# Two attention stages in one program, with the other batch's output and gated stages set between their steps

## The chip, the core and the metric

The kernel runs on one core of a Trainium2 chip. Its time is the device time of one execution in microseconds. The engines are TensorE (PE in the rows, its weight loads PEld), VectorE (DVE), ScalarE (ACT), GpSimd (POOL) and SyncE (SP, which issues most DMAs). They run side by side, each in its own order, and wait for each other by semaphores.

## What is computed

A tensor x of 2 batches x 1024 tokens x 512 features goes through four blocks, each `x = x + layernorm(block(layernorm(x)))`, with float32 in and out:

1. attention of 32 heads of 16, no mask: `softmax(q k^T / 4) v`, then `@ w_o`;
2. a gated feed-forward of width 1376 with integer weights and float scales: `(silu(x @ gate) * (x @ up)) @ down`;
3. attention of 32 query heads on one shared key and value head, with a causal mask and a slope per head, then `@ Wo`;
4. `z = x @ W + b` plus a low-rank product m, clipped by the ratio of their norms.

Attention and feed-forward of the first two blocks need nothing of the other batch. The projection of block 3 needs block 2 of its own batch alone.

## The kernel before

The program is a row of stages with a barrier after each: A (normalise, project q, k, v of block 1), B (attention 1), C (its output product, `output`), D (`gated_ffn`), F (projection for block 3), G (attention 2), H (its output product), I (`adapter_ffn`). Between stages the activations go through DRAM. Every product of float32 operands is three products of rounded parts (high x high, high x low, low x high, `split_product`, lines 73 to 75): a chain of 4 chunks x 3 is 12 matmuls of 128x128 weights by 512 columns into one PSUM bank. ScalarE makes the high parts, VectorE the low ones.

`attention` works on four heads of one batch at a time (16 such groups, `ITS`), in two halves of 512 queries ("turns", 32 in all) and, in a turn, in steps of 128 keys: 8 steps per turn in B (256 steps in all), 4 and 8 in causal G (192 steps). A step does this:

- `key_scores` (L793): the scores of 128 keys by 512 queries for 4 heads, one matmul each, into one of three banks `st_ps`. It uses only half of PE's rows: heads 0 and 1 lie in rows 0 to 63, heads 2 and 3 in rows 64 to 127, so two matmuls of different halves can run together. In G's diagonal steps two mask matmuls follow each (L804).
- `exps` (L720): ScalarE takes the exponential of each bank into `probs`.
- `values` (L826): the probabilities of the step before, times values with a column of ones, for 4 heads side by side in 32 columns each, summed in `o_ps`.
- `row_scores` (L782): the same scores with queries as rows, for a coming turn, into four banks `s_ps`, two per head and 128 queries; VectorE takes the maximum of each pair of banks in one scan (L755 in B, L752 with the mask in G). When a turn's maxima are there, PE turns them (L814), ScalarE and GpSimd split them in two parts and SP copies them as rows into `q_stack`.

The order within a step is planned in Python: `plan_units` spreads the scans over the steps in proportion to the work with a lead (`LEAD`), `step_order` alternates the two halves of PE's rows. On PE a step is: scores in that order, then the values of the step before.

C turns the outputs on PE (L894), scales by the sums, turns back (L902), splits, multiplies by w_o and normalises; D keeps all its split weights in SBUF and takes them once; F projects.

## Time and profile before

| | us |
|---|---|
| median of 3 runs (lowest, highest) | 2242.59 (2234.47, 2245.1) |
| the profiled execution | 2230.07 |
| its span, first to last instruction | 2228.3 |
| mean granted PE clock | 0.936 of full |
| PE, DVE, ACT, POOL busy | 1996.4, 1454.2, 1151.9, 134.4 |

The span falls into 0 to 221 us (A and the start of B up to its first step), 221 to 906 (B's steps), 906 to 1532 (C, D, F and the start of G), 1532 to 2016 (G's steps), 2016 to 2105 (H) and the rest (start and body of I). PE's busy time counts a matmul from issue to a modelled end, so neighbours overlap in it, and 99% busy is not the same as streaming all the time: the distance between starts says more.

### The profile page before, as it was taken

What the parts mean: (1) busy time and instruction counts of PE and PEld (TensorE: products, weight loads), DVE (VectorE), ACT (ScalarE), POOL (GpSimd) and SP (SyncE); (2) the same over time, 40 slices, a digit from 0 to 9 for tenths busy, and PEclk for the clock granted to TensorE, in tenths of its full rate; (3) what the DMA queues carried; (4) which work ended last, traced back from release to release, by engine and by line L of the source; (5) the groups of instructions that cost most, each with busy time, mean ns of one, the idle gap of its engine ahead of it and who ended that gap; (6) DMA issues with size and microseconds to landing.
All of it is one profiled execution on the core that took longest, in us unless ns stands there. A gap on an engine that the chain in (4) does not pass through costs nothing. (4 is left out here: it accounts for less than half of the span.)

```text
span 2228.3 us, 31983 instructions
## 1 busy us (share of the span) xinstructions
PE 1996.4 (90%) x12048; PEld 1151.6 (52%) x12048; DVE 1454.2 (65%) x2484; ACT 1151.9 (52%) x2431; POOL 134.4 (6%) x171
## 2 busy tenths in 40 slices
PE   7995999999999999869999998668999999998685
PEld 5772333333333333557888886454444444446564
DVE  5315899999999995464434233537777777835677
ACT  3220788888888887213322221223777777762153
POOL 0000000000000000120010010000000000001213
PEclk9995999999999999888999999786999999987898
DMA  6445233233233220244010100442332222202411
GB/s 220 161 147 73 35 53 45 39 50 48 39 49 49 39 35 2 76 146 127 17 38 1 39 19 5 169 125 49 50 49 46 42 42 46 50 2 95 147 45 69
DMA packets 97705, 143.57 MB, mean 64 GB/s; under 512 B 28900, under 2 KB 40036, under 8 KB 97408
## 3 DMA queue, kind: packets, MB, share of 16 engines
q1 hardware_dynamic: 96440, 139.35, 26.6%
q10 hardware_dynamic: 728, 1.41, 0.4%
q8 instruction: 95, 1.56, 0.3%
q0 software_dynamic: 384, 0.77, 0.2%
q14 instruction: 58, 0.48, 0.1%
HBM read 93.91 MB, written 47.05 MB: 63 GB/s over the span
## 5 line engine op out<-in xcount | busy, mean ns | idle before, releaser
L755 DVE TENSOR_REDUCE maxesB<-s_psB 128x1 f32<-128x1024 f32 x512 | 602.4, 1218 | 91.7 <-PE s_psB L782 91.6
L720 ACT ACTIVATE probsB<-st_psB 128x512 f32<-128x512 f32 x1024 | 529.0, 602 | 132.7 <-PE st_psB L793 132.6
L752 DVE CUSTOM_DVE_ANT_0 junkG<-s_psG,ramp 128x896 bf16<-128x896 f32 (+7 forms) x512 | 367.7, 755 | 120.2 <-PE s_psG L782 108.5
L793 PE MATMUL st_psB<-q_stackB,k_stackB 50*128 50x512 f32 x1024 | 410.5, 478 | 8.3 <-DMA q_stackB<-mpartsB 4.4
L720 ACT ACTIVATE probsG<-st_psG 128x512 f32<-128x512 f32 (+3 forms) x768 | 325.6, 492 | 115.8 <-PE st_psG L804 62.7
L782 PE MATMUL s_psB<-k_stackB,q_stackB 48*128 48x512 f32 x1024 | 354.8, 455 | 27.5 <-DMA k_stackB<-k_parts 20.5
L793 PEld LDWEIGHTS st_psB<-q_stackB,k_stackB 50*128 50x128 f32 x1024 | 169.8, 187 | 277.7 <-ACT probsB L720 235.4
L793 PE MATMUL st_psG<-q_stackG,k_stackG 54*128 54x512 f32 (+3 forms) x768 | 264.0, 419 | 22.2 <-ACT probsG L720 16.2
L782 PE MATMUL s_psG<-k_stackG,q_stackG 52*128 52x512 f32 (+3 forms) x768 | 255.8, 422 | 29.7 <-DMA q_stackG<-bias_copy 17.2
L826 PE MATMUL o_psB<-probsB,v_onesB 128*32 128x512 f32 x2048 | 279.3, 618 | 0.0
L782 PEld LDWEIGHTS s_psB<-k_stackB,q_stackB 48*128 48x128 f32 x1024 | 158.5, 191 | 116.9 <-DVE maxesB L755 86.7
L782 PEld LDWEIGHTS s_psG<-k_stackG,q_stackG 52*128 52x128 f32 x768 | 131.0, 193 | 117.0 <-DVE maxesG L752 69.7
L793 PEld LDWEIGHTS st_psG<-q_stackG,k_stackG 54*128 54x128 f32 x768 | 128.6, 189 | 110.9 <-ACT probsG L720 79.5
L826 PE MATMUL o_psG<-probsG,v_onesG 128*32 128x512 f32 (+3 forms) x1536 | 169.9, 516 | 0.0
L1128 DVE SCALAR_TENSOR_TENSOR hD<-u_psD,suD,siluD 128x512 f32<-128x512 f32 (+1 forms) x44 | 33.0, 750 | 203.0 <-PE u_psD L75 200.7
L804 PE MATMUL st_psG<-masks,halves 64*128 64x64 bf16 (+1 forms) x1024 | 120.6, 212 | 0.0
L1088 ACT ACTIVATE siluD<-g_psD,sgD 128x512 f32<-128x512 f32 (+1 forms) x44 | 30.3, 688 | 132.2 <-PE g_psD L75 132.1
L1096 ACT ACTIVATE hhD<-hD 128x512 fp32r<-128x512 f32 (+1 forms) x44 | 27.8, 632 | 118.4 <-DVE hD L1128 118.4
L826 PEld LDWEIGHTS o_psB<-probsB,v_onesB 128*32 128x32 f32 x2048 | 40.8, 109 | 64.7 <-ACT probsB L720 34.2
L73 PE MATMUL g_psD<-xhTD,wg_highD 128*128 128x512 f32 (+1 forms) x176 | 70.5, 400 | 1.4 <-DVE xlTD L170 1.4
L75 PE MATMUL g_psD<-xhTD,wg_lowD 128*128 128x512 f32 (+1 forms) x176 | 70.6, 401 | 0.0
L73 PE MATMUL y_psD<-wd_highD,hhD 128*128 128x512 f32 (+1 forms) x176 | 70.1, 398 | 0.0
(240 smaller groups left out, 2818.1 us busy)
## 6 DMA issues: line engine op xcount, KB each, us to landing
q_stackB<-q_parts SPq DMA_DIRECT2D x93, 128.0 KB
k_stackB<-k_parts SPq DMA_DIRECT2D x93, 128.0 KB
q_stackG<-q_parts SPq DMA_DIRECT2D x93, 128.0 KB
q_parts<-partsA SPq DMA_DIRECT2D x16, 512.0 KB, 2.8
k_parts<-partsA SPq DMA_DIRECT2D x16, 512.0 KB, 2.8
q_parts<-partsF SPq DMA_DIRECT2D x16, 512.0 KB, 2.8
k_stackG<-k_parts SPq DMA_DIRECT2D x93, 64.0 KB
xA<-in_x SPq DMA_DIRECT2D x4, 1024.0 KB
```

The source lines that it names most:

```text
L73: pe.matmul(out, left[0], right[0], start=start, stop=False)
L75: return pe.matmul(out, left[1], right[0], start=False, stop=stop)
L720: act.activation(probs[:, (i % ring) * GH + h, first:HALF], st_ps[:, n % n_st, first:HALF], ACT.Exp).then_inc(st_used, 1)
L752: dve.tensor_tensor_reduce(junk[:, n % JUNK, 0:width], scores, ramp[:, SEQ - width:SEQ], 1.0, LOWEST, ALU.add, ALU.max, out).then_inc(maxe ...
L755: dve.reduce_max(out, scores, AX.X).then_inc(maxed, 1)
L782: ins = pe.matmul(s_ps[:, slot_of[n] + part, 0:b - a], qst[at, it % 3, half, h % GS, qt * P:(qt + 1) * P], kst[at, it % 3, h % kh, a:b], s ...
L793: ins = pe.matmul(st_ps[:, n % n_st, first:HALF], kst[at, it % 3, h % kh, kt * P:(kt + 1) * P], qst[at, it % 3, half, h % GS, first:HALF], ...
L804: ins = pe.matmul(st_ps[:, n % n_st, first:first + wide], halves[at, a, :], masks[at, a, 0:wide], start=False, stop=a == 1)
L826: ins = pe.matmul(o_ps[32 * h:32 * h + 32, first:HALF], vone[:, it % 2, kt, h % vh, :], probs[:, (i % ring) * GH + h, first:HALF], start=k ...
L1088: act.activation(silu[0:k, :], g_ps[0:k, :], ACT.Silu, scale=sg[0:k, j:j + 1]).then_inc(silu_out, 1)
L1096: act.activation(hh[0:k, c % 2, :], h[0:k, :], ACT.Copy).then_inc(hh_out, 1)
L1128: dve.scalar_tensor_tensor(out=h[0:k, :], in0=u_ps[0:k, :], scalar=su[0:k, j:j + 1], in1=silu[0:k, :], op0=ALU.mult, op1=ALU.mult).then_in ...
```

## The change

Attention 1 and attention 2 become one list of 448 steps in one stage (`class Attention`): batch 0 and then batch 1 of block 1 (steps 0 to 127, 128 to 255), then batch 0 and batch 1 of block 3 (256 to 351, 352 to 447). Stages C (without its scaling), D and F are cut into units (`class Middle`): "o" one output tile, "t" turning a normalised tile, "g" and "u" a gate and an up product, "d" a group of up to four down products per 128 output columns, "b" turning the result back, "s" and "v" the second projection. A full unit is 12 matmuls. Per batch there are 8 o, 16 t, 22 g, 22 u, 24 d, 8 b, 10 s and 2 v. Batch 0's units stand in steps 140 to 230, batch 1's in steps 268 to 334, one or two per step in the first and one to three in the second.

In such a "filled" step PE does half of the scores, half of the unit products, the rest of the scores, the rest of the products, then the values. Eight PSUM banks are shared: in filled steps the row scores have two banks instead of four, the key scores two instead of three, the units three; each row scan is then two scans of 512 columns with a maximum to join them. `probs` holds two steps instead of four.

Further edits: the attention's outputs go to DRAM and come back packed, with reciprocals of the sums by two more DMA hops and a GpSimd product (`divide`), so nothing is turned on PE for it; silu is made from tanh in three operations; 1/sqrt is a power on GpSimd; gate, up, down and projection weights are fetched per use (82 pieces of 128 x 512 per batch, four landing places), converted to float and reduced to the low part on GpSimd and to the high part on ScalarE. H (`class Output`) is in the same program without a barrier before it, without the turning. A and I are as they were.

```diff
+FILLS = ((140, 231), (268, 318))
-JUNK = 8
+JUNK = 2
...
+        def give(key, ring, wide, release):
+            allowed = {"row": ([0, 1], [0, 1, 2, 3]), "take": ([4, 5], [4, 5, 6]), "fill": ([2, 3, 6],) * 2}[key[0]][not ring]
...
+            cuts = [(0, min(HALF, width)), (HALF, width)] if halved[t] else [(0, width)]
...
+class Middle:
+    def schedule(self, b, first, last):
+        order = [("o", b, t) for t in range(KT)] + [("t", b, 0, 0, i) for i in range(TB)]
...
+        for n, unit in enumerate(order):
+            early = after(unit)
+            if n >= 3:
+                old = mine[n - 3]
+                early = max(early, at[old] + (2 if old[0] in "ob" else 1))
...
+        elif kind in "gu":
+            ins = split_product(pe, bank[0:k_, :], self.parts(p, every, slice(k_ * g, k_ * (g + 1))),
+                                (self.xT[:, 0, g, :], self.xT[:, 1, g, :]), g == 0, g == n_groups - 1)
...
+        @block.vector
+            for i in range(steps):
+                early = att.scans_before_cut(i)
+                for n in early:
+                    att.maximum(dve, n)
+                mid.vector_middle(dve, i)
+                for n in att.scans_at[i][len(early):]:
+                    att.maximum(dve, n)
+                att.vector_step(dve, i)
+                mid.vector_last(dve, i)
...
+        @block.scalar
+            for i in range(steps):
+                mid.scalar_first(act, i)
+                att.exps(act, i, slice(0, GH // 2))
+                mid.scalar_middle(act, i)
+                att.exps(act, i, slice(GH // 2, GH))
+                att.scalar_step(act, i)
+                mid.scalar_last(act, i)
...
+        @block.tensor
+            for i in range(steps):
+                cut = att.cut_of(i)
+                att.scores(pe, i, slice(0, cut))
+                mid.front_products(pe, i)
+                att.scores(pe, i, slice(cut, None))
+                mid.back_products(pe, i)
+                if i:
+                    att.values(pe, i - 1)
+                for t in att.turn_after.get(i, ()):
+                    att.turn_max(pe, t)
```

PE in the middle of attention 1 before: `st_psB` are key scores, `s_psB` row scores, `o_psB` the values; one step from one L826 to the next.

```order
L826 MATMUL o_psB<-probsB,v_onesB 32x512 x4
L793 MATMUL st_psB<-q_stackB,k_stackB 128x512
L782 MATMUL s_psB<-k_stackB,q_stackB 128x512
L793 MATMUL st_psB<-q_stackB,k_stackB 128x512
L782 MATMUL s_psB<-k_stackB,q_stackB 128x512 x2
L793 MATMUL st_psB<-q_stackB,k_stackB 128x512
L782 MATMUL s_psB<-k_stackB,q_stackB 128x512
L793 MATMUL st_psB<-q_stackB,k_stackB 128x512
L826 MATMUL o_psB<-probsB,v_onesB 32x512 x4
```

The second half of a filled step of attention 1 now (its first half is a key score, a row score, a key score and six products like these); L971 are key scores, L959 row scores, L78 to L80 the products of one unit, L1007 the values.

```order
L80 MATMUL banks<-xT_mid,w_mid 128x512
L959 MATMUL banks<-k_stack,q_stack 128x512 x2
L971 MATMUL banks<-q_stack,k_stack 128x512
L959 MATMUL banks<-k_stack,q_stack 128x512
L971 MATMUL banks<-q_stack,k_stack 128x512
L78 MATMUL banks<-xT_mid,w_mid 128x512
L79 MATMUL banks<-xT_mid,w_mid 128x512
L80 MATMUL banks<-xT_mid,w_mid 128x512
L78 MATMUL banks<-xT_mid,w_mid 128x512
L79 MATMUL banks<-xT_mid,w_mid 128x512
L80 MATMUL banks<-xT_mid,w_mid 128x512
L1007 MATMUL banks<-probs,v_ones 32x512 x4
```

The four pairs of a step are cut into three and five matmuls with products between, and the three row scores of the second half stand close together, on two banks.

VectorE in attention 1 before (scans L755, the copy of a finished turn L759), and in filled steps now (scans L919; L1569 and L1595 the gate's and the up product's part of the activation, L1628 its low part).

```order
L755 TENSOR_REDUCE maxesB<-s_psB 128x1 x16
L759 COPY oTB<-o_psB 128x512
L755 TENSOR_REDUCE maxesB<-s_psB 128x1 x16
L759 COPY oTB<-o_psB 128x512
L755 TENSOR_REDUCE maxesB<-s_psB 128x1 x16
```

```order
L1569 SCALAR_TENSOR_TENSOR th_mid<-th_mid,banks 128x512
L919 TENSOR_REDUCE maxes<-banks 128x1 x3
L936 RECIPROCAL o_recip<-o_sums 128x16
L919 TENSOR_REDUCE maxes<-banks 128x1
L1595 SCALAR_TENSOR_TENSOR th_mid<-banks,sc_mid,th_mid 128x512
L919 TENSOR_REDUCE maxes<-banks 128x1 x3
L1628 TENSOR_TENSOR hx_1367<-th_mid,hx_1367 128x512
L919 TENSOR_REDUCE maxes<-banks 128x1
```

The unit's operation stands after the first of four half scans; its low part stands last in the step and waits for ScalarE.

At the end of attention 1 before, the steps have key scores alone, and stage C begins behind the barrier:

```order
L793 MATMUL st_psB<-q_stackB,k_stackB 128x512 x4
L826 MATMUL o_psB<-probsB,v_onesB 32x512 x4
L793 MATMUL st_psB<-q_stackB,k_stackB 128x512 x4
L826 MATMUL o_psB<-probsB,v_onesB 32x512 x8
L627 UNCONDITIONAL_BRANCH
L888 UNCONDITIONAL_BRANCH
L894 MATMUL a_psC<-ident,oTB 128x128 x16
```

The same place now carries the row scores of the first causal turn (narrow ones of 128 and 256 columns):

```order
L1007 MATMUL banks<-probs,v_ones 32x512 x4
L959 MATMUL banks<-k_stack,q_stack 128x512 x2
L959 MATMUL banks<-k_stack,q_stack 128x128
L971 MATMUL banks<-q_stack,k_stack 128x512
L959 MATMUL banks<-k_stack,q_stack 128x128 x2
L971 MATMUL banks<-q_stack,k_stack 128x512
L959 MATMUL banks<-k_stack,q_stack 128x128
L959 MATMUL banks<-k_stack,q_stack 128x256
L971 MATMUL banks<-q_stack,k_stack 128x512 x2
```

Attention 2 no longer starts from nothing.

## Rows read from the trace of the kernel before

**Rows 1.** The page: busy time and share of the span by engine.
```profile
PE 1996.4 (90%) x12048; PEld 1151.6 (52%) x12048; DVE 1454.2 (65%) x2484; ACT 1151.9 (52%) x2431; POOL 134.4 (6%) x171
```

**Rows 2.** Stretches by stage: length, then busy time (count) by engine, granted clock, DMA.
```profile
221.00:906.00 685.00, 676.52 (x4112) 247.14 (x4112) 591.95 (x521) 542.17 (x1086) 23.21 (x46) 0.98 0.28 40
906.00:990.00 84.00, 68.97 (x384) 58.04 (x384) 59.81 (x133) 16.20 (x37) 20.64 (x16) 0.94 0.31 109
...
1008.00:1392.00 384.00, 375.84 (x1632) 302.04 (x1632) 141.43 (x232) 98.17 (x138) 19.33 (x14) 0.98 0.10 30
...
1532.00:2016.00 484.00, 453.81 (x4108) 222.01 (x4108) 346.75 (x960) 351.56 (x862) 17.36 (x46) 0.97 0.24 41
2016.00:2105.00 89.00, 69.63 (x384) 59.23 (x384) 59.60 (x132) 16.80 (x38) 20.63 (x16) 0.88 0.31 109
```

**Rows 3.** Stretches inside the two attentions: steady part and tail of each.
```profile
400.00:500.00 100.00, 99.49 (x620) 36.79 (x619) 91.77 (x82) 80.69 (x163) 3.49 (x7) 1.00 0.30 45
...
866.00:904.00 38.00, 34.25 (x146) 9.44 (x142) 0.72 (x2) 23.80 (x48) 0.45 (x1) 0.70 0.00 1
...
1600.00:1700.00 100.00, 94.04 (x892) 47.57 (x891) 78.28 (x217) 74.59 (x187) 3.83 (x10) 1.00 0.35 54
...
1980.00:2015.00 35.00, 31.96 (x197) 11.76 (x196) 0.00 (x0) 19.48 (x48) 0.45 (x1) 0.65 0.00 1
```

**Rows 4.** Timeline of PE, one step of attention B (start, length, instruction).
```profile
601.23 0.49 PE L793 MATMUL st_psB<-q_stackB,k_stackB 50*128 50x512 f32 x1
601.23 0.49 PE L782 MATMUL s_psB<-k_stackB,q_stackB 48*128 48x512 f32 x1
601.56 0.39 PE L793 MATMUL st_psB<-q_stackB,k_stackB 50*128 50x512 f32 x1
...
602.41 0.49 PE L793 MATMUL st_psB<-q_stackB,k_stackB 50*128 50x512 f32 x1
602.83 0.64 PE L826 MATMUL o_psB<-probsB,v_onesB 128*32 128x512 f32 x4
603.28 0.61 PE L826 MATMUL o_psB<-probsB,v_onesB 128*32 128x512 f32 x4
603.82 0.50 PE L793 MATMUL st_psB<-q_stackB,k_stackB 50*128 50x512 f32 x1
```

**Rows 5.** Timeline of DVE, ACT and PE's loads in the same step.
```profile
601.76 2.07 ACT L720 ACTIVATE probsB<-st_psB 128x512 f32<-128x512 f32 x4 [0.53 <-PE st_psB L793]
...
601.84 0.18 PEld L782 LDWEIGHTS s_psB<-k_stackB,q_stackB 48*128 48x128 f32 x1 [0.31 <-DVE maxesB L755]
...
602.03 2.36 DVE L755 TENSOR_REDUCE maxesB<-s_psB 128x1 f32<-128x1024 f32 x2 [0.24 <-PE s_psB L782]
```

**Rows 6.** Groups by line and form: count, busy us, mean ns of one, idle before.
```profile
L755 DVE TENSOR_REDUCE maxesB<-s_psB 128x1 f32<-128x1024 f32 x512 | 602.4, 1218 | 91.7 <-PE s_psB L782 91.6
L1128 DVE SCALAR_TENSOR_TENSOR hD<-u_psD,suD,siluD 128x512 f32<-128x512 f32 (+1 forms) x44 | 33.0, 750 | 203.0 <-PE u_psD L75 200.7 <-ACT siluD L1088 2.3
L319 POOL TENSOR_TENSOR xD<-xD,yD 128x512 f32<-128x512 f32 x16 | 22.4, 1430 | 385.4 <-DVE yD L311 385.4
L752 DVE CUSTOM_DVE_ANT_0 junkG<-s_psG,ramp 128x512 bf16<-128x512 f32 x64 | 41.6, 689 | 13.6 <-PE s_psG L782 13.6
L678 POOL COPY v_onesB<-v_loadB 128x512 f32<-128x512 f32 x16 | 9.8, 616 | 115.0 <-PE o_psB L826 96.9 <-DMA v_loadB<-v_rows 18.2
L131 DVE TENSOR_SCALAR xnD<-xD,mvD,rstdD 128x512 f32<-128x512 f32 x16 | 7.7, 542 | 0.1
L311 DVE TENSOR_SCALAR yD<-yD,ymvD,yrstdD 128x512 f32<-128x512 f32 x16 | 15.4, 1024 | 0.1
```

**Rows 7.** Timeline of PE: 24 products apart, and 16 transposes at stage C's start.
```profile
154.89 0.39 PE L73 MATMUL acc_psA<-v_highA,xhTA 128*128 128x512 f32 x1
...
160.50 0.39 PE L73 MATMUL acc_psA<-v_highA,xhTA 128*128 128x512 f32 x1
...
906.97 1.94 PE L894 MATMUL a_psC<-ident,oTB 128*128 128x128 f32 x16 [1.60 <-PEq L1430]
```

More of the change, by code:

```diff
@@ new lines, in vector_step, with row_scores @@
+    def vector_step(self, dve, i):
+        t = self.ended(i, 1)
+        if t is not None and t < 2 * ITS:
+            self.vector_copy_o(dve, t)
+        t = self.ended(i, INVERT)
+        if t is not None:
+            self.invert(dve, t)
+    def row_scores(self, pe, n, part):
+        t, qt, h, *_ = self.scans[n]
+        it, half = divmod(t, 2)
+        a, b = self.scan_parts(n)[part]
+        if part == 0:
+            if t % 2 == 0 and (n == 0 or self.scans[n - 1][0] != t):
+                pe.wait_ge(self.stacks, self.stacks_by[it])
+            for free in self.frees["row", n]:
+                pe.wait_ge(*free)
+        at = slice(self.side(h), self.side(h) + MAIN + ALIBI)
+        ins = pe.matmul(self.banks[:, self.bank_of["row", n] + part, 0:b - a],
+                        self.qst[at, it % 3, half, h % GS, qt * P:(qt + 1) * P],
+                        self.kst[at, it % 3, h % GS if it < ITS else 0, a:b], start=True, stop=True)
+        if part == len(self.scan_parts(n)) - 1:
+            ins.then_inc(self.scored, 1)
@@ new lines, in key_scores @@
+    def key_scores(self, pe, i, h):
+        it, half, kt, first, diagonal = self.steps[i]
+        n = self.where["exp", i, h]
+        for free in self.frees["take", n]:
+            pe.wait_ge(*free)
+        at = slice(self.side(h), self.side(h) + MAIN + ALIBI + SHIFT)
+        ins = pe.matmul(self.banks[:, self.bank_of["take", n], first:HALF],
+                        self.kst[at, it % 3, h % GS if it < ITS else 0, kt * P:(kt + 1) * P],
+                        self.qst[at, it % 3, half, h % GS, first:HALF], start=True, stop=not diagonal)
+        if not diagonal:
+            ins.then_inc(self.st_made, 1)
@@ new lines, in values @@
+    def values(self, pe, i):
+        it, half, kt, first, _ = self.steps[i]
+        t = 2 * it + half
+        if i == self.first_of[t] and half == 0:
+            pe.wait_ge(self.v_set, it + 2)
+        if kt == 0 and t:
+            pe.wait_ge(self.o_out, t)
+        pe.wait_ge(self.st_used, max(self.exps_of[i]) + 1)
+        for h in range(GH):
+            ins = pe.matmul(self.banks[32 * h:32 * h + 32, 7, first:HALF], self.vone[:, it % 2, kt, h if it < ITS else 0, :],
+                            self.probs[:, i % 2 * GH + h, first:HALF], start=kt == 0, stop=i + 1 == self.first_of[t + 1])
+        ins.then_inc(self.pv_done, 1)
@@ new lines, in tensor_ahead, with scores @@
+    def tensor_ahead(self, pe):
+        pe.wait_ge(self.fixed, 16 * 2 * SIDES)
+        for n in self.before:
+            for part in range(len(self.scan_parts(n))):
+                self.row_scores(pe, n, part)
+        for t in self.early_turns:
+            self.turn_max(pe, t)
+    def scores(self, pe, i, items):
+        if items.start in (None, 0) and i == self.first_of[2 * self.steps[i][0] + self.steps[i][1]]:
+            pe.wait_ge(self.m_rows, self.N_ROWS * (2 * self.steps[i][0] + self.steps[i][1] + 1))
+        for kind, *which in self.orders[i][items]:
+            if kind == "row":
+                self.row_scores(pe, *which)
+            elif kind == "key":
+                self.key_scores(pe, i, *which)
+            else:
+                self.mask_keys(pe, i, *which)
@@ L1387, in one @@
         def one(i):
[L1388 removed]
+            return slice(i, i + 1)
         def store_parts(scratch, j):
```

1732 lines of the change are left out of this document (1062 added, 670 removed).

## The prediction

> **What bounds the kernel now.** I read the page first. PE is busy 90% of the span, DVE 65%, ACT 52%, POOL 6% [rows 1], so the time is PE's or that of whoever holds PE up. The stretches by stage come next [rows 2]: in attention B PE is busy 677 of 685 us, in D 376 of 384, in G 454 of 484, in H 70 of 89. Between C, D, F and G the barriers leave PE with little. Then the steady part of each attention [rows 3]. A step of B has 16.25 PE records (4 key scores, 4 row scores, 8 for the values, 2 per 8 steps for the turned maxima), so 620 in 100 us are 38.2 steps: 2.62 us per step. G has 260 records per 12 steps: 892 in 100 us are 41.2 steps: 2.43 us per step.
>
> The timeline of one step says how much of the 2.62 us PE needs [rows 4]. Two pairs of scores start 0.33 us apart, the last key score to the values takes 0.42, the two rounds of values 0.45 and 0.54: (603.82 - 602.83) = 0.99 us. Four pairs at 0.33, plus about 0.2 ahead of the values, plus 0.99 is 2.5 us. DVE has two scans in 2.36 us and ACT four exponentials in 2.07 [rows 5]. So there is 0.1 us of slack per step for foreign products, and 12 products between steps will lengthen them by nearly their whole length. The change can gain only what stands outside the steps, and it pays for cutting steps in two.
>
> **The cost of the units.** Products start 0.234 us apart at full clock: 24 in 160.50 - 154.89 = 5.61 us [rows 7]. A batch has 8 o + 22 g + 22 u + 16 full d + 10 s = 78 units of 12 and 8 of 9 products: 1008 products, 236 us. Its turning (t, b, v) is 104 small transposes at 1.94 / 16 = 0.12 us [rows 7]: 12.5 us. Together 248.5 us per batch, 497 for both.
>
> **The cost of a filled step of attention 1.** From the order on PE: first half, a pair (0.33), a key score alone (0.21) and a switch to the full array; six products; second half, two row scores (a pair), a key score, the third row score, the last key score; products; values 0.99. Two costs are new.
>
> First the third row score of the second half. It reuses the bank of the first one, whose scan must be over. From the issue of a row score to its scan: 602.03 - 601.56 = 0.47 us, the pair at 601.56 being the second of its head [rows 4, 5]. A scan of 512 columns was not run in B; the same width in G took 0.689 [rows 6], half of B's 1.218 would be 0.61; I take 0.69. From the end of a scan to the next load I take 0.04. So 1.20 us from the first row score to the third, and PE has two matmuls between them, 0.56 us: a stall of 0.64 us. Before, with four banks, the same wait was 0.31 us of a load whose neighbour went on [rows 5].
>
> Second the switches. The values use all rows in 32 columns, scores half the rows in 128 columns, products the whole array. The second round of values to the next score took 0.54 against 0.45 between the rounds: 0.09 us more; score to values took 0.42 against the 0.21 of its columns: 0.2 more [rows 4]. Before there are two such changes per step, now five. I take 0.1 for each added one, 0.3 per step; the ends are 0 and 0.6. The Trainium skill, TensorEngine Tiling (Array Packing), Key Properties, says that changing the tiling mode drains TensorE; by this rule the added changes cost something each, and the 0.09 and 0.2 agree.
>
> A filled step without its products is then 0.54 + 0.56 + 0.64 + 0.33 + 0.99 + 0.3 and the last key score's 0.1 of exposed load = 3.46 us, against 2.62. 91 steps: 315 us, plus 248.5 of units = 563; two more steps keep the narrow bank rings at about 3.2 us each: 6. 163 steps stay at 2.62: 427.
>
> **A filled step of attention 2.** Its scores are cut four and four with the pairs kept, its scans are short (128 to 512 columns), two row scores stand in each half and the first half's scans are over when six or more products have passed. I add 0.3 for switches and 0.07 for the rest: 2.8 us. 69 steps: 193 us, plus 248.5. Here a unit's bank is the one freed by the unit three before, and in 17 places that one stood in the step just before and is freed by an operation that DVE does only after this step's first scans: about 0.47 + 1.1 + 0.75 (the operation, 750 ns in D [rows 6]) against 1.0 of scores: 1.3 us each, 22; with smaller ones in the second halves 27. Sum 469. The other 123 steps at 2.43: 299.
>
> **What goes.** 906 to 1532 us (626 us: C, D, F, three starts behind barriers and G's start) go as a whole; their products are counted above. B's last 38 us hold 146 records, 12.2 steps of 12, worth 32 us; PE's granted clock was 0.70 there after it had less to do [rows 3]. These steps now carry the next layer's row scores at the full clock. Of the 14 us by which B's 685 exceed 256 steps at 2.62, I let 8 stand (the start). G's 484 exceed 192 steps at 2.43 by 17; its tail (35 us for 11.4 steps, clock 0.65 [rows 3]) stays, the start goes: 12 stand. H loses its turning and scaling and its start: 16 tiles of 12 products at 0.234 are 45 us, DVE needs about 2.7 per tile beside that, 8 us until the last turn's sums are back by DMA (DVE stands in line for them), 12 us from the last product to I's first work as now: 65 instead of 89. I's 123 us and A's 221 stay, with 5 more at the start, since SP alone issues all stacks and GpSimd more constant rows.
>
> **Cover.** Costs that I put at nothing, since PE has 6.2 us in a filled step of attention 1: DVE has four half scans (2.76) and on average 1.5 for units, ACT 2.07 and 1.1 for units and weights, POOL 0.9 pieces of a copy and a subtraction (616 ns for a copy, 1430 for a two-input operation [rows 6]): 1.8 and little else. Where POOL runs late, PE's wait for low weights is behind it, and everything in PE's order behind that. DMA brings 82 pieces of 0.26 MB in 569 us, 38 GB/s beside the 40 of attention B [rows 2]; stage C alone moved 109.
>
> **Sum.** 226 + 427 + 8 + 569 + 299 + 12 + 469 + 65 + 123 = 2198 us against 2228.3: 30 less, 1.3%. The profiled execution took 2230.07, 12.5 below the median of 2242.59; on the median's scale the forecast is 2212 us.
>
> **Rivals.** (a) PE hides its own waits. If the third row score's scan is earlier than I think (0.61 us scans, or a gap filled by reordered loads), switches cost nothing and bank waits vanish, then 58 + 47 + 27 = 132 us come off: 2080. For it: PE's loads are pulled ahead of waiting matmuls in rows 4 and 5. Against it: 0.20 before the values is in every step. Half of it gives 2146.
>
> (b) Slower: the hand-over of a filled step becomes a loop through three engines. h is made by DVE, its high part by ACT behind four exponentials, its low part by DVE as the last work of the step; the next step's first scan is behind that on DVE, and its end frees the bank that PE's second-half row score wants. By the durations above the low part ends 0.5 us before PE's next step, and another 1.0 us of lateness is absorbed until the second half. If DVE comes later than that, PE waits with it. An operation of POOL beside DVE's two-input one can do this: a `TENSOR_SCALAR` of 128x512 took 542 ns where GpSimd idles (L131) and 1024 where it adds rows at the same time (L311), though L311 also writes in place [rows 6]. One POOL operation of 1.43 us in the way of each step, 0.6 of it covered, is 0.8 x 158 = 126 us more: 2338. It decides from 0.19 us per filled step, where my 30 us are gone. The Trainium skill, SBUF — State Buffer, Who interferes with whom, says that a VectorE operation with two SBUF inputs and a GpSimd one that reads SBUF exclude each other for a whole instruction. By it L1628 would wait behind POOL's weight work; no run here shows this pair.
>
> (c) Weights come late. SP stands in one line for maxima, stacks, turns and 164 pieces, each piece needing the low part of the fourth before it. If each costs PE 0.5 us: 82 us more, 2294. For it: SP issues take 0.4 to 0.5 us and block on semaphores. Against it: pieces are asked for five steps ahead, some 30 us.
>
> That units aren't where they should be is excluded by the order.
>
> **Chances.** Forecast (2170 to 2250) 0.37; (a) 0.28; (b) 0.22; (c) 0.08; something else on the slow side 0.05. The range of 8 in 10 is 2100 to 2320. Within 0.5% (2231 to 2254), which a measurement of this kernel can't tell from no change, 0.15; faster 0.60 (all of (a), most of the forecast's width), slower 0.25.
>
> **What would show it.** In the changed profile: unfilled steps of 2.62 and 2.43 us; filled steps of attention 1 at 3.46 us plus 2.81 per unit; PE's waits for the scan before the third row score of 0.6 us about 90 times, some 58 us; no stretch of PE below full clock between the first step and attention 2's tail; H at about 65. Wrong: PE waiting for low weights (c), or DVE busy or waiting for ACT and POOL in filled steps with PE waiting for DVE over 1 us each (b), or filled steps near 2.9 us plus units (a).

## The result, and the profile after

The changed kernel took 2610.87 us (median of 4 runs, 2597.68 to 2615.69) against 2239.35 us for the kernel before (2234.47 to 2245.1): a ratio of 1.167, 95% interval 1.162 to 1.171. The forecast was 2212 us, the range 2100 to 2320, and slower had a chance of 0.25. It is 399 us off and outside the range. Now and then an execution takes clearly longer than the others of the same kernel; medians and ratios here leave such ones out.

The page of the changed kernel answers [rows 1]. The second row is the granted clock in 40 slices of the span:
```profile
PE 2205.2 (84%) x11728; PEld 1178.9 (45%) x11728; DVE 1488.7 (57%) x2924; ACT 1215.5 (47%) x2536; POOL 516.3 (20%) x624
PEclk9986999998699889987689889889978678785888
```
PE has fewer matmuls than before (11728 against 12048) and is busy 209 us longer. No other engine is near its limit. What differs is PE's clock: the mean granted clock is 0.866 against 0.936, and 704 us of the span lie at the level 0.5 (1.2 GHz), against 288 us before.

The stretches by stage answer [rows 2, 3]. They are, in this order: unfilled steps of attention 1, its filled steps, unfilled steps around the change to attention 2, filled steps of attention 2, its unfilled ones, H. Columns as in rows 2:
```profile
235.66:609.53 373.87, 361.02 (x2244) 133.28 (x2242) 336.64 (x326) 295.04 (x590) 23.59 (x35) 1.00 0.41 74
609.53:1326.77 717.24, 619.63 (x2625) 310.24 (x2624) 382.52 (x651) 304.90 (x574) 196.23 (x239) 0.86 0.27 61
1326.77:1433.21 106.44, 93.25 (x644) 39.98 (x642) 78.77 (x179) 72.82 (x156) 5.51 (x10) 0.91 0.41 87
1433.21:2005.68 572.47, 491.76 (x2608) 306.83 (x2606) 273.16 (x809) 222.84 (x489) 196.29 (x238) 0.88 0.29 70
2005.68:2417.34 411.66, 330.29 (x2360) 157.41 (x2362) 195.91 (x552) 208.05 (x498) 28.78 (x42) 0.73 0.29 59
2417.34:2490.00 72.66, 51.06 (x204) 36.46 (x196) 42.10 (x81) 11.65 (x18) 36.39 (x33) 0.85 0.27 95
```
Set beside the forecast's pieces, with the third stretch split at 1397.14 us, where attention 1's last values start. The same cuts, made at the first value product of a step, were made in the traces of the experiments below (one step later around the filled steps of e7, e10 and e12, whose units start later; the numbers hold to some 2 us). All in us of the profiled run; "at 0.5" is the time of the whole span at that granted clock:

| | forecast | after | e1 | e5 | e7 | e10 | e12 |
|---|---|---|---|---|---|---|---|
| start | 226 | 236 | 237 | 236 | 237 | 241 | 241 |
| attention 1, unfilled | 435 | 444 | 452 | 455 | 484 | 439 | 438 |
| attention 1, filled | 569 | 717 | 718 | 571 | 562 | 560 | 564 |
| attention 2, unfilled | 311 | 448 | 373 | 421 | 371 | 377 | 374 |
| attention 2, filled | 469 | 572 | 574 | 567 | 562 | 566 | 548 |
| H and I | 188 | 196 | 195 | 197 | 198 | 198 | 198 |
| sum | 2198 | 2614 | 2549 | 2446 | 2413 | 2381 | 2363 |
| at 0.5 | | 704 | 614 | 506 | 479 | 455 | 418 |

The surplus of 416 us has three main parts: 148 in the filled steps of attention 1, 137 in the unfilled ones of attention 2, 103 in its filled ones. They hold 200, 233 and 133 us of the time at 0.5.

**What a filled step does.** Four waits, over the whole span (waiting engine and line, what ended the wait, us in total, times, longest):
```profile
PE banks L959 <- DVE maxes L919: 93.0, 137, 4.1
PE banks L959 <- DVE maxes L916: 93.8, 48, 18.7
DVE o_recip L936 <- DMA o_sums<-turns: 139.0, 22, 26.6
PE banks L78 <- POOL w_mid L1452: 6.5, 2, 3.5
```
L959 is a row score, L919 and L916 are the scans of attention 1 and 2, L936 is `invert`, L1452 makes the low part of the weights. Of the first row 82.0 us lie in the filled steps of attention 1; of the third 94.6 us lie in attention 2's last unfilled steps. Step 174 of attention 1 shows the first row. PE's row scores, and DVE from the step's first scan to the last ones, from the timeline:
```profile
889.99 0.49 PE L959 MATMUL banks<-k_stack,q_stack 52*128 52x512 f32 x1
890.32 0.68 DVE L919 TENSOR_REDUCE maxes<-banks 128x1 f32<-128x512 f32 x1
890.92 0.67 DVE L1569 SCALAR_TENSOR_TENSOR th_mid<-th_mid,banks 96x512 f32<-96x512 f32 x1
891.06 0.50 PE L959 MATMUL banks<-k_stack,q_stack 52*128 52x512 f32 x1 [0.58 <-DVE maxes L919]
...
891.70 0.75 DVE L1595 SCALAR_TENSOR_TENSOR th_mid<-banks,sc_mid,th_mid 96x512 f32<-96x512 f32 x1
892.37 0.53 DVE L1611 TENSOR_SCALAR xn_mid<-x_mid,xmv_mid,xrstd_mid 128x512 f32<-128x512 f32 x1
892.82 1.96 DVE L919 TENSOR_REDUCE maxes<-banks 128x1 f32<-128x512 f32 x3
893.55 0.50 PE L959 MATMUL banks<-k_stack,q_stack 52*128 52x512 f32 x1 [2.00 <-DVE maxes L919]
...
895.32 0.79 PE L959 MATMUL banks<-k_stack,q_stack 52*128 52x512 f32 x1
```
The step's first scan stands ahead of DVE's work for the units, the other three behind it. The row score at 893.55 wants the bank of a row score whose scan is the first behind 1.9 us of unit work, and PE waits 2.00 us for it. The next row scores take 0.79 us instead of 0.50: the granted clock went to 0.5 at 894.6 and came back at 911.6. So a wait of 2 us was followed by 17 us at half the clock. That this wait alone lowered it isn't shown: the step holds only four transposes for its unit, and PE had been busy 7.34 of the 10 us before 894.
```profile
884.00:894.00 10.00, 7.34 (x39) 3.58 (x37) 5.61 (x10) 3.67 (x8) 1.50 (x3) 1.00 0.10 23
895.00:907.00 12.00, 10.35 (x36) 4.21 (x32) 7.45 (x12) 5.68 (x12) 1.72 (x4) 0.50 0.16 48
```

**What an unfilled step of attention 2 does.** Step 359, all of SP's turn work and what waits long (SPq rows are DMA issues):
```profile
2101.26 0.57 SPq L764 DMA_DIRECT2D o_packed<-turns  x1
2101.87 0.56 SPq L767 DMA_DIRECT2D o_sums<-turns  x1
...
2108.83 0.25 DVE L936 RECIPROCAL o_recip<-o_sums 128x16 f32<-128x16 f32 x1 [8.55 <-DMA o_sums<-turns]
...
2110.06 0.76 PE L959 MATMUL banks<-k_stack,q_stack 52*128 52x512 f32 x1 [7.78 <-DVE maxes L916]
```
DVE has come to the reciprocal at 2100.3, before the sums' fetch is issued, and goes on 7 us after the issue. The scans stand behind it in DVE's order, so PE waits 7.78 us. The two stretches around it, before and behind 2106 us:
```profile
2086.00:2106.00 20.00, 15.92 (x134) 8.17 (x129) 8.69 (x24) 10.95 (x30) 6.07 (x8) 0.83 0.32 68
2106.00:2140.00 34.00, 29.33 (x165) 14.14 (x166) 17.29 (x51) 14.43 (x32) 3.57 (x4) 0.55 0.16 34
```
34 us at 0.55 follow. The row of attention 2 in [rows 3] had 1.00.

### The profile page after: what moved, and what is told of

Its sections match the earlier page's. It is cut to its first block and busy times, and to the rows that moved or that the text cites. A ratio compares the mean times of both kernels' runs of the same rounds, so it can differ in the third digit from the quotient of the medians.

```text
span 2613.7 us, 34456 instructions
## 1 busy us (share of the span) xinstructions
PE 2205.2 (84%) x11728; PEld 1178.9 (45%) x11728; DVE 1488.7 (57%) x2924; ACT 1215.5 (47%) x2536; POOL 516.3 (20%) x624
## 5 line engine op out<-in xcount | busy, mean ns | idle before, releaser
L885 ACT ACTIVATE probs<-banks 128x512 f32<-128x512 f32 (+3 forms) x1792 | 887.5, 553 | 938.8 <-PE banks L971 616.4
L959 PE MATMUL banks<-k_stack,q_stack 52*128 52x512 f32 (+3 forms) x1792 | 686.0, 479 | 225.6 <-DVE maxes L916 93.8
L919 DVE TENSOR_REDUCE maxes<-banks 128x1 f32<-128x512 f32 (+1 forms) x720 | 630.8, 911 | 351.4 <-PE banks L959 350.4
L971 PE MATMUL banks<-q_stack,k_stack 54*128 54x512 f32 (+3 forms) x1792 | 751.4, 482 | 30.7 <-ACT probs L885 16.8
L916 DVE CUSTOM_DVE_ANT_0 junk<-banks,ramp 128x512 bf16<-128x512 f32 (+7 forms) x608 | 380.9, 660 | 374.8 <-PE banks L959 361.3
L959 PEld LDWEIGHTS banks<-k_stack,q_stack 52*128 52x128 f32 x1792 | 309.9, 206 | 489.7 <-DVE maxes L919 203.5
L971 PEld LDWEIGHTS banks<-q_stack,k_stack 54*128 54x128 f32 x1792 | 333.0, 208 | 382.4 <-ACT probs L885 213.7
L1007 PE MATMUL banks<-probs,v_ones 128*32 128x512 f32 (+3 forms) x3584 | 500.5, 635 | 0.0
L1452 POOL TENSOR_TENSOR w_mid<-land_mid,w_mid 128x512 fp32r<-128x512 f32 (+3 forms) x180 | 206.9, 1165 | 474.3 <-ACT w_mid L1531 474.0
L78 PE MATMUL banks<-xT_mid,w_mid 128*128 128x512 f32 (+1 forms) x432 | 196.8, 456 | 30.1 <-DVE th_mid L1595 13.9
L79 PE MATMUL banks<-xT_mid,w_mid 128*128 128x512 f32 (+1 forms) x432 | 180.4, 418 | 0.0
L80 PE MATMUL banks<-xT_mid,w_mid 128*128 128x512 f32 (+1 forms) x432 | 180.1, 417 | 0.0
L1007 PEld LDWEIGHTS banks<-probs,v_ones 128*32 128x32 f32 x3584 | 74.1, 113 | 120.2 <-issue 77.1
L78 PEld LDWEIGHTS banks<-xT_mid,w_mid 128*128 128x128 f32 (+1 forms) x432 | 86.1, 199 | 83.9 <-issue 32.1
L80 PEld LDWEIGHTS banks<-xT_mid,w_mid 128*128 128x128 f32 (+1 forms) x432 | 87.0, 201 | 21.7
L936 DVE RECIPROCAL o_recip<-o_sums 128x16 f32<-128x16 f32 x64 | 15.9, 248 | 139.0 <-DMA o_sums<-turns 139.0
L79 PEld LDWEIGHTS banks<-xT_mid,w_mid 128*128 128x128 f32 (+1 forms) x432 | 87.2, 202 | 14.2
L78 PE MATMUL banks<-hx,w_mid 128*128 128x512 f32 (+1 forms) x176 | 83.1, 472 | 12.0 <-DVE xT_mid L1582 4.9
```

Source lines behind the costliest of these rows:

```text
L78: pe.matmul(out, left[0], right[0], start=start, stop=False)
L79: pe.matmul(out, left[0], right[1], start=False, stop=False)
L80: return pe.matmul(out, left[1], right[0], start=False, stop=stop)
L885: act.activation(self.probs[:, i % 2 * GH + h, first:HALF], self.banks[:, self.bank_of["take", n], first:HALF], ACT.Exp).then_inc(self.st_ ...
L916: dve.tensor_tensor_reduce(self.junk[:, n % JUNK, 0:b - a], scores, self.ramp[:, SEQ - width + a:SEQ - width + b], 1.0, LOWEST, ALU.add, A ...
L919: dve.reduce_max(out, scores, AX.X).then_inc(self.maxed, 1)
```

## The experiments

Times are medians, ratios are to the kernel before on the same chip. The kernel before took 2231 to 2236 us in them.

**e1: the sums are not waited for.** One operand and one wait of `invert`; the products are then divided by wrong sums.
```diff
-        dve.wait_ge(self.s_moved, 16 * (t + 1))
+        dve.wait_ge(self.v_set, 1)
...
-        dve.reciprocal(self.fewer[:, t % 2, :], self.few[:, t % 2, :])
+        dve.reciprocal(self.fewer[:, t % 2, :], self.fixed_sums[:, :])
```


> The changed kernel with one data dependence left out: DVE's reciprocal reads a constant tile of ones and no longer the sums that come back by DMA, so its outputs lack the division by the right sums. Every store, fetch, reciprocal and copy of the round trip is still issued. Theory 1 (DVE stands in order for the sums' DMA, 139 us in 22 waits; PE then waits for scans; after each stall PE runs for 10 to 17 us at the granted clock 0.5): the waits and most of the 231 us at low clock in the unfilled steps of attention 2 go; these 123 steps fall from 449 to 300-330 us, the whole to 2330-2420. Theory 2 (filled steps and sparse units lower the clock by themselves, the waits for the sums only stand where PE was late anyway): filled attention 1 stays at 700 or more, the whole stays above 2480. Theory 3 (SP is late with stacks, maxima and weights): little changes, 2550 or more.

Measured: 2550.93 us, ratio 1.143 (1.136 to 1.151). My first theory explains 60 us of the 370, against the 190 to 280 that it expected. It is right about its place: attention 2's unfilled steps fell from 448 to 373 us, and their low clock with them:
```profile
616.76:1334.90 718.14, 621.04 (x2625) 310.79 (x2625) 382.39 (x651) 304.79 (x574) 195.49 (x238) 0.86 0.27 60
2017.11:2353.67 336.56, 296.46 (x2360) 146.77 (x2362) 197.07 (x553) 204.70 (x498) 28.83 (x42) 0.84 0.35 72
```
The first row, the filled steps of attention 1, is what it was (717.24 and clock 0.86): the larger surplus is there, and it is not the sums.

**e2: the reciprocal later.** Whole computation.
```diff
-STORE_TURN, FETCH_TURN, INVERT, STORE_INVERSE, SPREAD_INVERSE, DIVIDE = 2, 4, 6, 7, 9, 11
-FILLS = ((140, 231), (268, 318))
+STORE_TURN, FETCH_TURN, INVERT, STORE_INVERSE, SPREAD_INVERSE, DIVIDE = 2, 4, 9, 10, 11, 13
+FILLS = ((142, 231), (270, 315))
```


> The whole computation. The reciprocal stands 9 steps behind the end of a turn instead of 6 (store of it 10, spread 11, division 13; the units of each batch start 2 steps later). Theory 1: the fetch is issued early enough in SP's order for most turns, so the waits for the sums fall from 139 to under 40 us and the time to 2350-2450. Theory 2: above 2500. Theory 3 (SP itself is behind by more than three steps): the waits move with it, above 2550.

Measured: 2563.7 us, ratio 1.146 (1.139 to 1.153), within its noise of e1. The two are made up differently: in e2 some 55 us of waits for the sums are left (28 of them in the last one), attention 2's unfilled steps fell as in e1 (374 us), attention 1's filled ones came to 697, and its unfilled ones rose from 444 to 489. The value I gave theory 1 was wrong in both.

**e3: the sums in the products' layout.** The stores and spreads of the inverses are gone, DVE inverts 128x512 elements once per two turns.
```diff
-        sp.dma_start(self.few[:, t % 2, :], ...)
+        sp.dma_start(self.inverse[at, slot, :], self.turns[t].rearrange("h s c q -> s h c q")[1])
...
-        dve.reciprocal(self.fewer[:, t % 2, :], self.few[:, t % 2, :])
+        dve.reciprocal(self.inverse[:, slot, :], self.inverse[:, slot, :])
```


> The whole computation with a shorter round trip: the sums, which stand 16 times in the turn anyway, are fetched in the layout of the products, DVE inverts them there 9 steps behind the turn (32 times 128x512, some 0.6-3 us each, instead of 64 times 128x16), and the stores and spreads of the inverses are gone (128 DMAs fewer for SP). Theory 1: waits for the sums under 20 us, 2330-2430. Theory 3 (SP's line): a gain as well, but without one in e1 and e2. Theory 2: above 2500. If the reciprocal of 128x512 takes 3 us, 32 times 2.5 us more of DVE show as stalls and give back up to 80 us.

Measured: 2645.27 us, ratio 1.186 (1.177 to 1.195), slower than the changed kernel. The new operation costs 3.35 us, where 16 columns took 0.25:
```profile
L926 DVE RECIPROCAL o_inverse<-o_inverse 128x512 f32<-128x512 f32 x32 | 107.1, 3346 | 54.6 <-DMA o_inverse<-turns 54.6
```
Its 107 us stand for the 16 us of the 64 small ones, 91 more; against e1 it lost 94. It can't say what the shorter trip is worth.

**e4: a pause in the kernel before.** Attention 2 of the kernel before, 15 times.
```diff
+                if causal and n and n % (2 * UNITS) == 0:
+                    for j in range(7):
+                        dve.reduce_max(spare[:, at + j:at + j + 1], ramp[:, :], AX.X)
                 dve.wait_ge(scored, n + 1)
```


> The kernel before, whole computation, with a pause of DVE of seven 1024-wide maxima of a constant tile (about 8.4 us by the 1.218 us of such a scan in attention 1) at the first scan of every tile pair of attention 2: 15 pauses, once per 12 steps, as often as the changed kernel stalls there. Its own price, less some slack: 7 us each, 105 in all, so 2345 if a stall costs only its length. Theory 1 (the granted clock falls to 0.5 after a stall and stays there 10 to 17 us): 4 to 7 us more behind each, 2400-2450, with stretches at 0.5 behind each pause. Theory 2 (the clock is lowered by what the changed kernel's steps are like): no fall of the clock here.

Measured: 2408.53 us, ratio 1.078 (1.073 to 1.084): 177 us, 11.8 per pause. One pause, and the stretch of attention 2 that holds nearly all of them:
```profile
1660.82 7.97 DVE L750 TENSOR_REDUCE spareG<-ramp 128x1 f32<-128x1024 f32 x7
...
1669.05 0.58 PE L787 MATMUL s_psG<-k_stackG,q_stackG 52*128 52x256 f32 x1 [7.57 <-DVE maxesG L757]
```
```profile
1555.00:2130.00 575.00, 453.11 (x3551) 226.43 (x3548) 428.53 (x964) 310.23 (x739) 15.20 (x40) 0.77 0.19 32
```
The same attention in the kernel before:
```profile
1555.00:1990.00 435.00, 407.91 (x3813) 202.71 (x3812) 331.47 (x912) 323.24 (x796) 16.23 (x43) 1.00 0.25 42
```
PE's wait is 7.6 us, the price 11.8. Over the whole span PE's waits for these scans rose from 9.1 to 116.5 us, 107 of the 177; the other 70 go with the time at 0.5, which rose from 27 to 279 us in attention 2. So a wait costs its length and then the low clock behind it, in a kernel that has nothing of the change, though 70 us for 252 more us at the low level is less than the half that a clock at half speed could cost.

**e8: a short pause.** As e4 with three maxima, 3.6 us.

> The kernel before, whole computation, with three instead of seven maxima in each of the 15 pauses of DVE (3.4 us each by their own rows in e4; e4's of 8.0 us cost 11.8 us each). Attention 2 has some 0.4 to 1 us of slack per pause. If a stall of PE of 2.5 to 3 us also lowers the clock for some microseconds, the cost is 4 to 7 us each, 60 to 105 us, so 2290-2335; if only long stalls do it, 2.5 us each: 2265-2275.

Measured: ratio 1.054 (1.047 to 1.061), some 120 us or 8 per pause of 3.6; its four runs lay between 2342 and 2424 us, wide apart, so only the rough size (7 us per pause even by the shortest) is to be taken from it. It is over both expectations: the price of a pause is about double its length. Short waits are not cheap ones.

**e5: two row scores on each side of the units.** The cut of a filled step moves one item on, behind the second row score; DVE's unit work then stands behind two scans. Whole computation.
```diff
-        return [n for n, item in enumerate(order) if item[:1] + item[2:] == last][GH // 2 - 1] + 1
+        cut = [n for n, item in enumerate(order) if item[:1] + item[2:] == last][GH // 2 - 1] + 1
+        rows = [n for n, item in enumerate(order) if item[0] == "row"]
+        if len(rows) == 4 and sum(n < cut for n in rows) == 1 and rows[1] == cut:
+            cut += 1
+        return cut
```


> The changed kernel, whole computation; in a filled step of four half scans the cut moves behind the second row score (two row scores and their scans stand ahead of the units, two behind, instead of one and three), so that no row score waits for a scan that stands behind DVE's unit work. Theory 4 (short waits of 0.6 to 2 us of PE for the scans inside filled steps, each followed by 3 to 10 us of granted clock 0.5): PE's waits for the scans of attention 1's filled steps fall from about 79 us to under 25, low clock there from 200 us to about 100, the whole by 90 to 130 us: 2480-2525. Theory 5 (PE's clock falls in steps that hold only transposes or nothing, whatever the waits): the waits go but the low clock stays, 2550-2590. The sums' round trip (theory 1, worth 58 us by e1) is left as it is.

Measured: 2449.88 us, ratio 1.097 (1.094 to 1.100): 161 us off, over theory 4's own expectation. PE's waits for the scans in the filled steps of attention 1, in the changed kernel and in e5 (L919 has become L923), and e5's stretch of these steps:
```profile
PE banks L959 <- DVE maxes L919: 82.0, 101, 4.1
```
```profile
PE banks L963 <- DVE maxes L923: 9.8, 15, 2.9
```
```profile
615.14:1185.71 570.57, 537.33 (x2625) 280.16 (x2624) 372.25 (x651) 295.65 (x574) 195.44 (x238) 0.95 0.34 76
```
The same 2625 matmuls in 571 instead of 717 us, the clock at 0.95 instead of 0.86. The waits are 72 us shorter. The time at 0.5 fell from 200 to 58 us, which at half speed is worth up to 71: together 143 of the 147. Theory 5 expected the low clock to stay. It went, though the steps that hold only transposes are still there, so these steps don't lower the clock by themselves; e6 shows that they have a part in it.

**e6: more work for PE.** 20 constant bf16 products ahead of the transposes of each of the 48 turning units.
```diff
+            self.extra(pe, bank)
             for c in range(DC):
                 ins = pe.transpose(bank[:, P * c:P * (c + 1)], self.xn[:, n % 2, P * c:P * (c + 1)], self.ident[:, :])
```


> The changed kernel, whole computation, with work added: 20 products of a constant bf16 tile (128x128 by 128x256, an estimate from the mask products' rows is 0.11 us each at full clock) ahead of the transposes of each of the 48 units that only turn a tile, some 2.2 us each, 105 us of PE work in all, where PE's steps are sparse. Theory 5: the clock stays up there, steps of 7.8 us at half clock become 6.2, and the whole comes out at or under 2614 in spite of the added work (2570-2620). Theory 4: the waits for scans are partly filled by the products (they let DVE catch up), so the added work costs 20 to 60: 2630-2670. If clock and waits are untouched: 2700 or more.

Measured: 2613.26 us, ratio 1.170 (1.165 to 1.176): 960 more matmuls, and no difference from the changed kernel. That is theory 5's expectation (2570 to 2620), and under theory 4's. Five steps with a transposed tile or nothing (146 to 150), of the changed kernel and then of e6:
```profile
672.03:710.00 37.97, 28.07 (x103) 10.19 (x106) 23.54 (x46) 14.58 (x29) 10.88 (x14) 0.55 0.30 43
```
```profile
674.80:708.50 33.70, 27.27 (x179) 14.62 (x178) 22.86 (x45) 13.96 (x27) 10.87 (x14) 0.95 0.31 41
```
With 76 more matmuls recorded they take some 4 us less, at 0.95 instead of 0.55. DVE's work is the same. All filled steps of attention 1, and PE's waits for the scans in them:
```profile
610.89:1319.77 708.88, 619.45 (x3105) 337.36 (x3104) 382.13 (x651) 304.11 (x574) 195.69 (x238) 0.95 0.27 61
```
```profile
PE banks L959 <- DVE maxes L919: 72.7, 99, 2.4
```
The waits are nearly all there (72.7 us of 82.0), and the clock stands at 0.95, as in e5. So the waits for the scans alone don't lower the clock either: taking them away (e5) keeps it up, and so does filling the sparse steps around them (e6). And e6 gives the clock's price by itself. Its time at 0.5 in this stretch fell by 136 us, worth up to 68; its 480 added products are some 53 us by the 0.11 expected of each; measured, 8 us less. In attention 2's filled steps the same sum is 31 against 53, and they got 19 us longer.

**e7: e2 and e5 together.** No new edit.

> The whole computation with e2's later reciprocal and e5's cut together. If the two causes stand side by side their gains add: 2610 - 50 - (e5's gain); by theory 4 2430-2475, by theory 5 2500-2540.

Measured: 2419.98 us, ratio 1.086 (1.081 to 1.090). The gains do not quite add: 30 us beyond e5, where e2 alone had given 47. Attention 1's filled steps stand at 562 us, but its unfilled ones rose to 484, since PE now waits for the maxima's rows (`q_stack<-mparts`), 35.1 us in 10 waits against 10.0 in 7 in e5.

**e10: scans further ahead.** e7 with a longer lead of the scans in attention 1.
```diff
-        ... + (rate * LEAD if t else 0)
+        ... + (rate * (5200 if layer == 0 else LEAD) if t else 0)
```


> Whole computation: e7 (2420), and in attention 1 the scans run further ahead of the steps (5200 columns instead of 3400, some two steps more), so that the maxima's rows have 5 us more to travel. e7's trace has the first step of 7 turns at 5.8 to 7.8 us instead of 2.62, PE waiting up to 5 us for the DMA of the maxima's rows, and low clock behind them. If these waits are that trip: 163 unfilled steps of attention 1 fall from 481 to 435-445 us and the whole to 2375-2390. If they follow the reciprocal, not the rows: 2415-2425.

Measured: 2381.54 us, ratio 1.069 (1.064 to 1.074), as expected: 439 us unfilled, and 4.4 us of waits for these rows.

**e9: GpSimd inverts.** e5 with e3's layout, and a power of -1 on GpSimd in the place of DVE's reciprocal.
```diff
+        pool.tensor_tensor(self.inverse[:, slot, :], self.inverse[:, slot, :], self.minus[:, :].broadcast_to([P, HALF]), ALU.pow)
```


> Whole computation, with e5's cut. As in e3 the sums are fetched in the layout of the products and the stores and spreads of the inverses are gone (128 DMAs fewer), but GpSimd takes them to the power -1 ahead of its multiplication; DVE has no part in the division. 32 operations of 128x512 on GpSimd, whose duration no row shows (128x1 took 0.55 us). Against e5 (2450): if the power takes under 5 us, DVE's wait goes and SP is relieved, 2370-2410; if it takes 10 us or more it stands ahead of GpSimd's weight work and maxima, and the time is over 2450.

Measured: 4583.94 us, ratio 2.054 (2.049 to 2.060). One such operation takes 82 us:
```profile
L833 POOL TENSOR_TENSOR o_inverse<-o_inverse,minus 128x512 f32<-128x512 f32 x32 | 2621.5, 81922 | 67.9 <-DMA o_inverse<-turns 67.9
```
It says nothing on SP's relief.

**e11: stacks of the second batch early.** e7, with attention 2 of the second batch reading the first one's parts.
```diff
-            if it >= ITS and it % NG == 0:
+            if it == ITS:
...
-                return k_parts[1][c, one(it // NG % BATCH)].rearrange("b d (j t) -> (b d) j t", j=1)
+                return k_parts[1][c, one(0)].rearrange("b d (j t) -> (b d) j t", j=1)
...
-            late = {ITS + NG * b: mid.ends[b] + 3 for b in range(BATCH)}
+            late = {ITS: mid.ends[0] + 3}
```


> e7 with one dependence left out: attention 2 of the second batch reads the first batch's parts, so its stacks can be loaded early (its output is wrong). e7's trace has two stalls in the unfilled steps, 16.9 us at step 339 and 17.8 at 351, with PE waiting for the DMA of k_stack, and 32 us at low clock around them. If the late projection of the second batch is the cause: both steps fall to 2.5-4 us, 29 us and some clock, 2380-2395 against 2420. If SP's line is: it stays within 10 us of 2420.

Measured: 2414.96 us, ratio 1.084 (1.080 to 1.088), 5 us from e7. The stall of step 339 went (16.9 to 4.0 us), that of step 351 stayed (16.4 us, PE waiting 12.0 for `k_stack`). So the first of the pair hangs on the late projection. The second doesn't; that it hangs on when SP loads the next stack is likely, but no run shows it. Attention 2's unfilled steps got some 15 us shorter, and attention 1's unfilled steps and H 10 us longer; why wasn't followed.

**e12: one unit behind three.** e10, in 15 steps.
```diff
         half = (len(todo) + 1) // 2
+        if len(self.at(i)) == 1 and len(self.at(i - 1)) >= 3:
+            half = 0
```


> Whole computation: e10 (2382), and in the 15 steps of attention 2 that hold one unit behind a step of three, all its 12 products stand in the second half of the step. e10's trace has such a step (288) at 9.35 us against 5.61: PE waits 2.3 us for DVE's third gating operation, which frees the last of the three unit banks, and runs 3.4 us at the granted clock 0.5 behind it. If that hand-over is what makes attention 2's filled steps 97 us longer than forecast: PE's waits before L78 there fall by 20 to 25 us, low clock from 142 to about 100, and the whole to 2335-2350. If the low clock comes from the rest of the steps, the waits go and come back later: 2370-2385.

Measured: 2371.84 us, ratio 1.061 (1.058 to 1.064). That is the second of the two outcomes I had written down: some waits go and others come. The filled steps of attention 2 fell from 566 to 548 us. In e10, step 288 shows the wait that was removed:
```profile
1442.99 0.50 PE L78 MATMUL banks<-xT_mid,w_mid 128*128 128x512 f32 x1 [2.30 <-DVE th_mid L1599]
1443.33 0.40 PE L79 MATMUL banks<-xT_mid,w_mid 128*128 128x512 f32 x1
...
1444.28 0.63 PE L79 MATMUL banks<-xT_mid,w_mid 128*128 128x512 f32 x1
```
PE's waits for `th_mid` in this stretch fell from 17.7 to 4.9 us, but those for the scans and for ACT rose by 11 us together. Some 80 us above the forecast stay there: 66 us of waits, where the forecast had 27, and 113 us at the low clock. The waits are short, up to 2.9 us, and spread over several releasers; no run takes them away.

**e13: e12 and 12 added products per turning unit.**

> Whole computation: e12 with 12 of e6's constant products (about 0.11 us each) ahead of the transposes of each of the 48 turning units, 63 us of added PE work. In e6 such steps stayed at full clock at 5.2 to 6.2 us with 20 products. If PE's idle time there is a fall of the clock waiting to happen: 10 to 30 us less than e12, 2310-2335. If e5's cut has already taken away what lowered the clock there, the added work only costs: 10 to 40 us more than e12.

Measured: 2391.38 us, ratio 1.070 (1.066 to 1.075): about 20 us more than e12 for some 60 us of work. Time at 0.5 fell from 418 to 352 us, the time didn't. Once e5's waits are gone, the clock that useless work holds up pays back two thirds of the work and no more.

No version came under the kernel before. The fastest, e12, does the changed kernel's work in 239 us less.

## Why the prediction was wrong

- **Start and H.** 236 against 226, H and I 196 against 188. Right to 20 us together.
- **Unfilled steps of attention 1.** 444 against 435: right.
- **A filled step of attention 1 as such.** Forecast 3.46 us and 2.81 per unit. Without the 0.64 us for the third row score that is 5.63 us for a step with one unit and 8.44 with two. With that wait taken out, e5 and e7 measured 5.5 and 8.2 us in such steps where the clock was full. So the order, the switches together and the products were priced right; that e7 and e10 came to 562 and 560 us, near the 569, is partly chance, since 58 us of the 569 are a stall that they don't have, and other waits and 48 us at the low clock took its place. The term of 0.64 us was not right: the same steps of the changed kernel took 6.5 and 9.25 us at full clock, 1.0 more. I took the distance between two row scores, with a scan that starts at once. I wrote in the same part that DVE has 1.5 us of unit work per step and put it at nothing under "Cover", without asking where in DVE's order it stands. It stands between the first scan and the three others. 82 us of waits instead of 58, the longest 4.1; with other waits, which the forecast had at nothing, PE stood 98 us in these steps.
- **The clock.** This is the step that failed. The prediction prices waits at their length and says "no stretch of PE below full clock between the first step and attention 2's tail". [Rows 3] already showed the other side: the tails of both attentions, where PE's load has holes, ran at 0.70 and 0.65. I used this row to give the tail back at full clock and not to charge the holes that I was adding. The low clock rose from 288 to 704 us. At half speed that is up to 208 us of the 385 between the two profiled runs, and e5 shows 161 us for the removal of 72 us of waits. An estimate for the filled steps of attention 1: 40 us more of waits than forecast and half of 200 us at 0.5 are 140 of the 148.
- **The sums.** The prediction names DVE's wait for the last turn only (8 us in H). The same in-order wait stands behind each of the 64 turns: 139 us in 22 waits, 94.6 of them in attention 2's last unfilled steps. e1 puts them, with what follows them, at 60 us of the whole. They are not all of the 137 us there: e12 still takes 374 us against 311, with 34 us of waits for the DMA of `k_stack` in 8 waits. Two steps at which the changed kernel took 12.4 and 4.7 us (339 and 351) take 15.7 and 18.2 us in it: behind the repaired wait another one appears. My note that SP issues every DMA alone was attached to weights, where nothing happened (PE waited 6.5 us for low weights), and not to the fetches, where it did.
- **Filled steps of attention 2.** The place was named: a unit's bank freed by DVE behind the step's first scans, 17 places at 1.3 us. Measured 2.3 us at step 288 of e10 and 3.4 us at the low clock behind it, but in the changed kernel's whole stretch only 18 us for `th_mid`: this term was not too small. The others were missing: PE stood 80 us in all against 27 forecast, and 133 us lie at 0.5, up to 67 of them lost. e12 gets 18 of the 103 us back; the rest is read from the trace, and no run shows it.
- **Rivals.** (b) had the right side and the right engine, PE waiting for DVE with unit work in its order, and the wrong price: 2338. Its mechanism, DVE held by GpSimd, is there but small. The prediction had no run with this pair; the changed kernel has it. 39 of the 44 L1628 took 664 to 695 ns. The other five took 0.88 to 2.26 us, each begun while a GpSimd operation ran on for another 0.3 to 1.05 us; the one at 730.40 ended 0.55 us behind the GpSimd operation it had met. Together they cost DVE 3.4 us, since GpSimd was rarely at work at that moment. (c) as a wait for weights is refuted by the 6.5 us. (a) is refuted: PE's waits for the scans did not vanish.

The Trainium skill, TensorE: Matmul & The Clock Gate, A second HAM failure mode: psum-queue depth-cycling, tells of a kernel where TensorE idles briefly between groups of matmuls, cycling through PSUM banks, and loses throughput to repeated throttling. This trace agrees: PE's 137 waits for a bank that L919 frees were at most 4.1 us long, and the 704 us at the low level are 59 stretches, one of them the 17 us behind the wait at 893.55 us. The Trainium skill, TensorE: Matmul & The Clock Gate, Loop structure matters more than you think, has a copy out of PSUM by VectorE as harmless for the clock in a loop whose next matmuls follow at once. Here PE had to wait for VectorE's maximum of a bank, so that case was not given, and without 72 us of these waits the time at 0.5 fell from 200 to 58 us (e5).

## What to carry to other kernels

When a change puts foreign work into a loop that PE fills to 99%, write down for each engine in which order its instructions then stand, and look at what is behind the foreign ones: some 1.9 us of DVE work ahead of the scans, put at nothing in the forecast, was worth 161 us (e5). Price a wait of PE at its length and again for the clock: in e4 7.6 us of waiting cost 11.8, in e5 72 us gave 147 back in their stretch. The second part hangs on how full PE is around the wait (e6). A DMA that an in-order engine needs for its next small step belongs well behind its issue (five steps in e2, two before), or its wait stops everything behind it. Then look for the next wait: with the sums' wait gone, step 351 went from 4.7 to 18.2 us (e12).

## What the runs showed of the hardware

- Three maxima of 1.2 us in DVE's order, 15 times, cost some 8 us each, seven of them 11.8: the price fell far less than the length (e8, e4).
- The same five steps ran at 0.55 with 103 PE records and at 0.95 with 179 (e6), and were some 4 us shorter.
- With PE's waits for scans nearly unchanged (72.7 us against 82.0), added products took the time at 0.5 in one stretch from 200 to 64 us (e6).
- DVE's reciprocal took 0.25 us for 16 columns and 3.35 us for 512, 6.2 ns for each further one (e3); a scan of 512 took 0.69 us.
- GpSimd's power took 0.55 us for one column and 82 us for 512 (e9).
- A VectorE operation with two SBUF inputs (L1628), begun while a GpSimd operation that reads SBUF ran on for another 0.3 to 1.05 us, took 0.88 to 2.26 us instead of 0.69, five times of 44.
- A fetch of the sums was issued at 2101.87 us and let DVE go on at 2108.83, 7 us later, beside the stack loads.
